# Second expert layer turned over (512 tokens move past w2 in split fp32r passes), scores spread by DMA, and batch 0's gate within attention step 15

## What is computed

```python
x = x + attention(ctx, layernorm(x))            # two batches of 512 tokens
x2 = layernorm(x)
probs = softmax(x2 @ Wg)                        # 8 experts
top_vals, top_idx = top_k(probs, 2)             # normalised to a sum of 1
scores = sum(onehot(top_idx) * top_vals)        # [tokens, 8], 6 of 8 are zero
h = relu(x2 @ W1[e] + b1[e])                    # per expert, 128 -> 256
y = h @ W2[e] + b2[e]                           # per expert, 256 -> 128
out = x + sum_e(y * scores[e])
```

## Time and profile before

| | |
|---|---|
| median of 3 runs | 345.25 us (345.12 to 345.28) |
| the profiled execution | 345.45 us, its span 343.7 us |
| busy: TensorE, VectorE, GpSimd, ScalarE | 98%, 79%, 74%, 56% of the span |
| granted TensorE clock | 1.00 of full |

### The profile page before, as it was taken

How to read it: one execution, slowest core, us unless ns; L and a number is a source line. 1 busy time by engine, 2 the same in 40 slices (tenths; PEclk the granted TensorE clock), 3 DMA queues, 4 the chain that set the end, 5 groups by cost and what they waited for, 6 DMA issues and landing times.

```text
span 343.7 us, 6136 instructions
## 1 busy us (share of the span) xinstructions
PE 336.9 (98%) x2355; PEld 231.9 (67%) x2355; DVE 270.7 (79%) x430; ACT 193.7 (56%) x257; POOL 254.1 (74%) x163
## 2 busy tenths in 40 slices
PE   7899999999999999999999999999999999999996
PEld 7576657584757566575847475665684478999896
DVE  5989757988999999999879897979728898267333
ACT  2564768484948566584849485665803544045341
POOL 4639999999999999999999899989883772110000
PEclk9999999999999999999999999999999999999999
DMA  4630000000010000000000000000000010000000
GB/s 126 212 97 0 2 0 4 0 17 0 2 31 17 15 2 0 3 1 2 0 17 2 1 0 17 0 2 0 2 3 0 1 32 0 2 0 2 31 3 31
DMA packets 6713, 5.81 MB, mean 17 GB/s; under 512 B 743, under 2 KB 5789, under 8 KB 6685
## 3 DMA queue, kind: packets, MB, share of 16 engines
q1 hardware_dynamic: 6389, 5.29, 5.0%
q10 hardware_dynamic: 296, 0.13, 0.1%
HBM read 4.89 MB, written 0.52 MB: 16 GB/s over the span
## 4 chain that ended last, share of the span: by engine, by line
PE 96%; ACT 2%; DVE 1%; issue 0%; POOL 0%; DVEq 0%; POOLq 0%
PE xo L415 25%; PE sc L395 21%; PE mx L617 8%; PE sc L401 6%; PE sc L321 6%; PE sc L322 5%; PE sc L323 5%; PE mx L352 3%; PE xo L352 3%; PE mx L504 2%; PE xo L504 2%; PE sc L436 2%; PE xo L424 2%; PE mx L321 1%; PE mx L322 1%; PE mx L323 1%
## 5 line engine op out<-in xcount | busy, mean ns | idle before, releaser
L1142 POOL TENSOR_TENSOR psum_acc<-psum_acc,probs 111x1024 f32<-111x1024 f32 x63 | 161.6, 2565 | 9.3 <-DVE psum_acc L864 1.9
L686 ACT ACTIVATE probs<-sc 111x1024 f32<-111x1024 f32 x96 | 98.2, 1027 | 19.0 <-PE sc L401 12.4
L415 PE MATMUL xo<-probs,v_sb 111*64 111x512 f32 x384 | 88.2, 596 | 0.0
L395 PE MATMUL sc<-q_pair,k_pair 64*111 64x512 f32 x576 | 86.0, 402 | 0.8 <-ACT v_sb L676 0.4
L395 PEld LDWEIGHTS sc<-q_pair,k_pair 64*111 64x111 f32 x576 | 44.7, 171 | 29.0 <-issue 12.2
L415 PEld LDWEIGHTS xo<-probs,v_sb 111*64 111x64 f32 x384 | 26.2, 137 | 42.3 <-issue 38.7
L875 DVE RECIPROCAL recips<-recips 128x128 f32<-128x128 f32 x64 | 54.0, 905 | 0.0
L841 DVE TENSOR_REDUCE part_max<-mx 128x2 f32<-128x888 f32 x32 | 34.7, 1083 | 18.3 <-PE mx L352 16.9
L1142 POOL TENSOR_TENSOR psum_acc<-probs 111x1024 f32<-111x1024 f32 x16 | 38.4, 2401 | 8.9 <-ACT probs L686 8.9
L702 ACT COPY recips<-xo 128x512 f32<-128x512 f32 x16 | 9.4, 587 | 56.7 <-PE xo L424 48.8
L401 PE MATMUL sc<-max_row,ones_r 64*111 64x512 f32 x192 | 38.2, 390 | 0.0
(11 more groups left out here) (179 smaller groups left out, 522.1 us busy)
## 6 DMA issues: line engine op xcount, KB each, us to landing
w_raw<-in_L_ffn_W SPq DMA_DIRECT2D x8, 128.0 KB, 2.3
x_tok<-in_x SPq DMA_DIRECT2D x2, 256.0 KB, 3.1
wv_raw<-in_L_xattn_Wkv SPq DMA_DIRECT2D x4, 128.0 KB, 2.8
wout_sb<-in_L_xattn_Wout SPq DMA_DIRECT2D x1, 512.0 KB
wqk_raw<-in_L_xattn_Wq SPq DMA_DIRECT2D x7, 64.0 KB, 1.9
wqk_raw<-in_L_xattn_Wkv SPq DMA_DIRECT2D x7, 64.0 KB, 2.4
out<-x_tok SPq DMA_DIRECT2D x1, 256.0 KB, 2.0
out<-x_tok SPq DMA_DIRECT2D x2, 128.0 KB, 1.7
```

The costliest lines, as they stand in the source:

```text
L395: pe.matmul(sc[0:KP, kt % 2, h, :], k_pair[r, s % QKB, k_part, at], q_pair[r, s % QKB, q_part, :], start=(k_part + q_part == 0), stop=False)
L415: mm = pe.matmul(o_ps[h * HD:(h + 1) * HD, :], v_sb[0:KP, s // 2 % 2, kt, at:at + HD], probs[0:KP, e % RING, h, :], start=(kt == 0), stop= ...
L686: act.activation(probs[0:KP, e % RING, :, :], sc[0:KP, kt % 2, :, :], ACT.Exp).then_inc(exp_done, 1)
L1142: pool.tensor_tensor(psum_acc[0:KP, s % 2, :, :], first, probs[0:KP, e % RING, :, :], ALU.add) \
```

## The change

The second expert layer is turned over. Before, the hidden tokens stood still and w2 moved; now parts of w2 stand still and 512 hidden tokens move, in fp32r. For that w2 is split into a high and a low part (ScalarE's `w2_high` in steps 11 to 14 into the buffers of the attention's weights, GpSimd's `w2_low`), and so is the hidden layer: for each expert ScalarE does `relu_first`, `high_first`, `relu_second`, `high_second`, GpSimd `low_first` and VectorE `low_second`. `layer_two(g)` is six passes of 512 columns, three for each half, and runs two experts behind `layer_one` (`LAG`).

The result now has features on partitions and tokens along the row, so the scores must be spread over all partitions: the turned scores go to DRAM (`score_rows`) and come back by eight DMAs, one per expert, each reading one row of 2 KB for 128 partitions (`spread`). `add_expert` is a multiplication (out of PSUM, into `scaled`) and an addition (both inputs in SBUF) of 128x512. At the end of a batch `turn_acc` transposes the sum back and `add_rows` adds it to x. The bias term is one matmul of 512 columns and enters with the first expert's addition.

Batch 0's gate moves into step 15: `turn_x2(0)` stands ahead of the dots of step 15 and `logits(0)` behind them, the transposes of the scores behind layer one of expert 0. VectorE leaves the reciprocals of steps 12 and 13 out of step 14, so that x1 comes first, and does them and those of 14 and 15 later; all five gathers of step 15 are GpSimd's. w1's high parts move from GpSimd to ScalarE, all of w1 is split by step 13. Of batch 1, `turn_scores(1)` stands at g = 10, `bias_term(1)` at 11, and `turn_acc` of batch 0 at 12. `out_project(1)` runs at g = 3 (seven pairs) and 4 (the last).

```diff
-W1_AT = {2: 0, 3: 1, 9: 2, 11: 3}
+W1_AT = {2: 0, 3: 1, 8: 2, 9: 3, 10: 4, 11: 5, 12: 6, 13: 7}
+W2_HI_AT = {11: (0,), 12: (1, 2), 13: (3, 4), 14: (5, 6, 7)}
 FR = 6
+LAG = 2
...
+        relu_ring = sb("relu_ring", [P, 2, N])
+        relu_lo = sb("relu_lo", [P, FR, N], F32R)
+        spread = sb("spread", [P, E, N])
+        relu_hi = sb("relu_hi", [P, FR, N], F32R)
...
+        score_rows = nc.dram_tensor("score_rows", (B, E, N), F32, kind="Internal").ap()
...
+            for b in range(B):
+                sp.wait_ge(score_copied, b + 1)
+                if b == 0:
+                    sp.wait_ge(added, (KT - 1) * STEPS)
+                sp.dma_start(score_rows[b], score_t[:, b, :]).then_inc(rows_out, 16)
+                sp.wait_ge(rows_out, 16 * (b + 1))
+                for e in range(E):
+                    if b:
+                        sp.wait_ge(y_scaled, e + 1)
+                    sp.dma_start(spread[:, e, :], score_rows[b, e].partition_broadcast(P)).then_inc(spread_in[e], 16)
+            sp.wait_ge(out_ready, 1)
...
+                pe.matmul(pj, b2_sb[:, :], score_t[:, b, :], start=True, stop=True).then_inc(bias_ready, 1)
...
+            def layer_two(g):
                 e = g % E
                 if g >= 2:
-                    pe.wait_ge(acc_v, QT * (g - 1))
+                    pe.wait_ge(y_scaled, g - 1)
+                elif g == 1:
+                    pe.wait_ge(score_copied, 1)
+                if g == B * E - 1:
+                    pe.wait_ge(r0_done, g)
+                pe.wait_ge(w2_split, min(g + 1, E))
+                for half, at in enumerate(halves if g == B * E - 1 else [slice(0, N)]):
+                    y = y_ps(g, half)[:, at]
+                    for c, hi_done, lo_done in ((0, hi0_done, lo0_done), (1, hi1_done, lo1_done)):
+                        n = (g * HC + c) % FR
+                        pe.wait_ge(hi_done, g + 1)
+                        pe.matmul(y, w2_hi(e)[:, c, :], relu_hi[:, n, at], start=(c == 0), stop=False)
+                        pe.matmul(y, w2_lo(e)[:, c, :], relu_hi[:, n, at], start=False, stop=False)
+                        pe.wait_ge(lo_done, g + 1)
+                        mm = pe.matmul(y, w2_hi(e)[:, c, :], relu_lo[:, n, at], start=False, stop=(c == HC - 1))
+                    mm.then_inc(y_ready, 1)
...
+            turn_x2(0)
             s = STEPS - 1
             for kt in range(KT):
                 dots(s, kt)
+            logits(0)
             pe.wait_ge(sum_copied, s - 1)
             total(s - 1)
-            for kt in range(3):
+            for kt in range(KT):
                 pv(s, kt)
-            turn_x2(0)
-            for kt in range(3, KT):
-                pv(s, kt)
-            logits(0)
             for g in range(B * E):
-                hidden(g)
+                layer_one(g)
+                if g == 0:
+                    turn_scores(0)
                 if g == 1:
+                    bias_term(0)
                     pe.wait_ge(o_copied, STEPS)
                     total(s, o_ps)
-                if g >= 1:
-                    expert_out(g - 1)
-                if g == 2:
+                if g == 10:
+                    turn_scores(1)
+                if g >= LAG:
+                    layer_two(g - LAG)
+                if g == 3:
                     pe.wait_ge(sum_copied, STEPS)
-                if g % E == 2:
-                    turn_scores(g // E)
-                if g % E == 3:
-                    bias_term(g // E)
+                    pe.wait_ge(o_norm, STEPS - 1)
+                    out_project(1, x1_ps[1], range(PAIRS - 1))
                 if g == 4:
-                    pe.wait_ge(score_copied, 1)
-                    out_project(1, x1_ps[1], range(PAIRS))
+                    pe.wait_ge(o_norm, STEPS)
+                    out_project(1, x1_ps[1], range(PAIRS - 1, PAIRS))
                 if g == 6:
                     turn_x2(1)
                 if g == 7:
                     logits(1)
-            expert_out(B * E - 1)
+                if g == 11:
+                    bias_term(1)
+                if g == 12:
+                    turn_acc(0, 0, range(QT))
+            for g in range(B * E - LAG, B * E):
+                layer_two(g)
+            for half in range(2):
+                turn_acc(1, half, range(2 * half, 2 * half + 2))
...
+            def relu_first(g):
+                if g >= 2:
+                    act.wait_ge(hi0_done, g - 1)
+                    act.wait_ge(lo0_done, g - 1)
+                relu(g, 0, relu_ring[:, g % 2, :], r0_done)
+
+            def high_first(g):
+                act.wait_ge(r0_done, g + 1)
+                if g >= 3:
+                    act.wait_ge(y_ready, g - 2)
+                act.copy(relu_hi[:, g * HC % FR, :], relu_ring[:, g % 2, :]).then_inc(hi0_done, 1)
+
+            def relu_second(g):
+                relu(g, 1, hid_ps[:, (g * HC + 1) % 4, :], r1_done)
+
+            def high_second(g):
+                act.wait_ge(r1_done, g + 1)
+                if g >= 3:
+                    act.wait_ge(y_ready, g - 2)
+                act.copy(relu_hi[:, (g * HC + 1) % FR, :], hid_ps[:, (g * HC + 1) % 4, :]).then_inc(hi1_done, 1)
...
-            copy_x2(0)
+                act.copy(score_t[:, b, :], score_ps[b][0:E, :]).then_inc(score_copied, 1)
+
+            gate_exp_of(0)
             copy_output(STEPS - 1)
-            gate_exp_of(0)
             act.wait_ge(added, (KT - 1) * (STEPS - 1) + 1)
             for g in range(B * E):
-                for c in range(HC):
-                    relu(g * HC + c)
+                relu_first(g)
+                high_first(g)
+                relu_second(g)
+                high_second(g)
+                if g in (0, 10):
+                    copy_scores(g // E)
                 if g == 1:
                     copy_sum(STEPS - 1, o_ps)
-                if g % E == 2:
-                    copy_scores(g // E)
                 if g == 6:
-                    copy_x2(1)
-                if g == 7:
+                    copy_x2()
+                if g == 8:
...
-                if s > HALVED:
-                    for c in range(RC):
-                        reciprocal(s - 1, c)
...
+            def low_second(g):
+                dve.wait_ge(hi1_done, g + 1)
+                if g >= 3:
+                    dve.wait_ge(y_ready, g - 2)
+                dve.tensor_tensor(relu_lo[:, (g * HC + 1) % FR, :], hid_ps[:, (g * HC + 1) % 4, :],
+                                  relu_hi[:, (g * HC + 1) % FR, :].bitcast(F32), ALU.subtract).then_inc(lo1_done, 1)
+
+            def add_expert(g, half=0, at=slice(0, N)):
                 b, e = g // E, g % E
-                dve.wait_ge(y_ready, g + 1)
-                if e >= 1:
-                    dve.wait_ge(acc_v, QT * g)
+                dve.wait_ge(y_ready, g + half + 1)
+                dve.wait_ge(spread_in[e], 16 * (b + 1))
+                if g == 0:
+                    dve.wait_ge(sum_ready, STEPS)
+                if g >= 2:
+                    dve.wait_ge(acc_v, g - 1)
+                dve.tensor_tensor(scaled[:, g % 2, at], y_ps(g, half)[:, at], spread[:, e, at], ALU.mult) \
+                   .then_inc(y_scaled, 1)
+                dve.wait_ge(y_scaled, g + half + 1)
+                if e == 0:
+                    dve.wait_ge(bias_ready, b + 1)
                 else:
-                    dve.wait_ge(score_ready, b + 1)
-                for t in range(QT):
-                    if g == B * E - 1 and t == 2:
-                        dve.wait_ge(y_ready, g + 2)
-                    dve.scalar_tensor_tensor(acc[:, b, t, :], y_ps(g, t)[:, t * P:(t + 1) * P],
-                                             score[:, b, t, e:e + 1], acc[:, b, t, :], ALU.mult, ALU.add) \
-                       .then_inc(acc_v, 1)
+                    dve.wait_ge(acc_v, g)
+                dve.tensor_tensor(acc_t(b)[:, at], scaled[:, g % 2, at], acc_t(b)[:, at] if e else pj,
+                                  ALU.add).then_inc(acc_v, 1)
...
             norm_x1(0)
-            gather(STEPS - 1, 3)
+            for c in range(RC):
+                reciprocal(STEPS - 4, c)
             split_x2(0)
             for c in range(RC):
-                reciprocal(STEPS - 2, c)
+                reciprocal(STEPS - 3, c)
             gate_start(0)
             gate_end(0)
+            dve.wait_ge(added, (KT - 1) * (STEPS - 1) + 1)
             for g in range(B * E):
-                add_expert(g)
+                low_second(g)
+                if g == 5:
+                    norm_x1(1)
                 if g < 2:
                     for c in range(2 * g, 2 * g + 2):
+                        reciprocal(STEPS - 2, c)
+                if g >= LAG:
+                    add_expert(g - LAG)
+                if g in (2, 3):
+                    for c in range(2 * g - 4, 2 * g - 2):
                         reciprocal(STEPS - 1, c)
-                if g % E == 3:
-                    add_bias(g // E)
-                if g == 3:
```

(42 more changed lines are left out.)

197 lines of the change are left out of this document (110 added, 87 removed).

## The result

The changed kernel takes **365.09 us** (median of 4 runs, 364.34 to 366.09) beside 345.26 for the kernel before in the same runs: ratio 1.0569, 95% interval 1.0548 to 1.059. Forecast were 358.4, from 348 to 363. The direction was right, the time lies 2 us above the range. The profiled execution took 365.76 us, its span is 364.0, 7.2 more than the 356.8 of the sum.

The account below looks back on a forecast made before the run. TensorE, busy 98% of the span, was taken as the bound. 340.3 us with nobody late plus waits of 7.2, 3.4, 1.8, 3.8 and 0.3 gave 356.8 of span; + 1.55 made 358.4 us, range 348 to 363.

Parts of the forecast that it names:

- the 356.8 of the sum: Whole kernel: span of 340.3 us with nobody late plus TensorE's forecast waits, 7.2 + 3.4 + 1.8 + 3.8 + 0.3.
- The mechanism that decides: Batch 0's gate in step 15: VectorE operations stand behind GpSimd's gathers, scores at 285.3, TensorE stands 7.2 us.
- no standing at the port: Rival, chance 0.15: short VectorE operations slip between GpSimd's, batch 0's gate ends at 276.6, time 348.2 us.
- Second layer and transposes: TensorE's experts: layer two 1.39 us for 1.78, 6.2 us off in all; turning batch 0's sum back costs 0.44.
- The bias term: On TensorE: one 512-wide matmul, two records of 0.215 us, replaces 1.08 us; 1.3 us off for both.
- The tail: After layer one of expert 15 (T): ScalarE, VectorE's last sums, transposes and store end at T + 10.7, 340.3 us.
- the span with nobody late: Whole kernel if no engine delays another: 340.3 us, which is 343.7 - 3.4.
- Batch 1's x1 and logits: TensorE waits 3.4 us before x2's transposes, norm tiles standing behind GpSimd low parts, and 1.8 us before the logits.
- Batch 1's scores: Before the scores' transposes TensorE stands 3.8 us; the gate takes 4.1 us and one standing, to 329.9.
- The spreads: Batch 1's scores through DRAM to all partitions take 5.2 to 6.6 us; TensorE waits 0.3 us (0 to 0.8).
- spreads are slow: Rival, chance 0.06: one-row reads for 128 partitions take twice the landing time, 3.1 us more in batch 1, about 361.5.
- a rival with 0.20: Chance 0.20: after TensorE's 7 us standing, pieces behind run at 1.2 GHz, up to 4.2 us more, 360.5 to 362.6.

Follow-up runs that it names:

- the last three kernels: Three edits plus both gates in PSUM, batch 1's cut in two, 346.39 us; then VectorE's last steps reordered, 345.57; then bias term and step 15's sum moved, 344.8.
- the tail turned round: Against the kernel with both gates in PSUM: at g = 14 and 15 VectorE multiplies the expert two back before the newest low part, adds behind; 345.57 us.
- the last version: Against the kernel with VectorE's last steps reordered: bias term and sum of step 15 moved behind the first second layer; 344.8 us, ratio 0.9982.
- the three-edit kernel: Changed kernel with batch 0's gate in PSUM, GpSimd held back from batch 1's norm tiles, x2's low part ahead of expert 6's; 352.46 us, ratio 1.0177.
- the first experiment: Changed kernel with 26 identity matmuls on TensorE ahead of the wait for batch 0's scores; 361.46 us, ratio 1.0464.

## Why the prediction was right in direction and short in size

*The mechanism that decides was right.* Forecast: VectorE's two-input SBUF operations in the gate stand until GpSimd's are over, gate some 13 us, TensorE 7.2 us idle. Measured: 12.4 and 6.50. The gate in PSUM takes 4.2 us in the same place, beside the same gathers. The Trainium skill ("SBUF — State Buffer", Who interferes with whom) tells of such a standing between these two engines; the trace agrees, with 12.4 us against 4.2. The rival *no standing at the port* (348.2) fell with it.

*Second layer and transposes* were right: 1.39 us an expert (351.07 to the start of the next piece at 352.46 by six records 0.23 apart), 0.44 for the transposes back.

*The bias term* was not. "Two records of 0.215" were to take 0.43 us in place of 1.08; the two records take 1.05 (342.48 to 343.53 above), so 0.03 is saved each time where 1.3 us were booked for the two. It is an fp32 matmul of 8 rows, and it was priced by the passes of layer one, which are fp32r; no run tells its type from its few rows.

*The tail* was T + 10.1 for T + 10.7 (353.9 to 364.0), 0.6 the other way. So the span with nobody late, forecast 340.3, is 341.0 in the kernel after and in the one with both gates in PSUM: right within 0.7, in part because two errors of opposite sign nearly cancel.

*Batch 1's x1 and logits*: 2.92 for 3.4 and 1.04 for 1.8; the tiles stood, 3.45 against 1.11.

*Batch 1's scores* were mis-sized: 5.25 for 3.8. The step gave the gate 4.1 us and one standing. In the trace it starts at 330.00, 0.5 before TensorE asks, and takes 5.67, because two of its operations stand beside expert low parts of GpSimd, 0.84 and 1.37:

```profile
330.43 0.84 DVE L1089 TENSOR_TENSOR g_prob<-g_exp,g_rec 128x32 f32<-128x32 f32 x1
...
332.50 1.37 DVE L1099 TENSOR_TENSOR g_eq<-g_eq,earlier 128x256 f32<-128x256 f32 x1
```

```profile
329.74 1.48 POOL L1265 TENSOR_TENSOR relu_lo<-relu_ring,relu_hi 128x512 fp32r<-128x512 f32 x1 [2.44 <-ACT relu_hi L871]
...
332.15 1.44 POOL L1265 TENSOR_TENSOR relu_lo<-relu_ring,relu_hi 128x512 fp32r<-128x512 f32 x1 [0.94 <-ACT relu_hi L871]
```

*The spreads* cost TensorE nothing in the changed kernel (forecast 0.3): the store of the scores is issued at 337.38, the first product starts at 342.07 and VectorE stands 3.88 us for it, but the low clock had made TensorE late too. With the clock up they cost 0.59 to 0.79 in the last three kernels. The rival *spreads are slow* had part of its premise right, 5.2 us from issue to landing for the 3.1 of the model, and no weight in the time.

*The step that failed* is the sum's: "340.3 + 7.2 + 3.4 + 1.8 + 3.8 + 0.3 = 356.8" holds no term for the clock. It stood beside as a rival with 0.20 and 2 to 4 us, on the ground that "nothing in rows speaks for it yet". The runs put in its place 5.25 us in batch 0 and 2.0 in batch 1, both removed where TensorE was kept busy. Two things were wrong in that rival besides its chance. It stopped at "layer one, bias, sum, layer one, 4.2 us" of work, where the low level lasted through 6.05 us of work by full clock (11.3 less 5.25), since bias term and sum did not bring it back. And it reckoned with one fall, although the sum had a second wait of 3.8 us. The Trainium skill ("TensorE: Matmul & The Clock Gate", Part 1: The HAM clock gate) was cited there; it sides with what the windows show, an array that stood being set back to the lower level and working there first. With 7.3 added, the sum gives 364.1 us of span beside 364.0. That it fits so well is luck in part: the waits were 0.8 shorter than forecast (15.71 for 16.2 + 0.3) and the tail 0.6, the bias terms 1.3 longer.

What the change is worth without its waits is 2.7 us of span (343.7 less 341.0), where 3.4 were forecast; the tail turned round takes 0.6 more. The kernel with both gates in PSUM gives all of it back to its waits of 2.75; the last version gets 0.6.

Open is why a wait of 2.9 us at x2 left the clock up in the kernel after and in the one with bias term and sum moved (both behind an earlier fall) and brought it down in three others, and whether the second group of runs at 347 is the fall behind the bias term that the trace of the three-edit kernel shows. No run of that group was profiled; that the group is gone when the two pieces are moved speaks for it, and so do its mean clocks (0.993 to 0.995 beside 0.996 to 1.0), while the 1.55 us that such a fall cost is less than the 2.5 by which the group is slower.

## What to carry to other kernels

A wait of several microseconds on TensorE is to be priced twice: the wait, and the work behind it at half clock until the granted clock is back, which light pieces put right behind the wait draw out (11.3 us against 4.6). A matmul is to be priced by a row of its own type and shape: two records of 512 columns took 0.46 us in layer one and 1.05 in the bias term. Short VectorE operations with both inputs in SBUF should not be set beside long GpSimd operations; with one input in PSUM they run undisturbed. A saving on the bounding engine reaches the end only if the engines that hand to it have the time to spare, so before taking 7 us from TensorE count how late each hand-over becomes, in a row, since a wait that is removed shows up again at the next one.

## What the hardware showed that was not expected

- The granted clock fell without any long wait: behind 0.60 us of waiting, the bias term of 8 rows and the sum of step 15 (1.12 and 1.08 us), to 0.50 from 283.2 to 286.9 in the three-edit kernel. In the kernel with batch 0's gate in PSUM alone the same pieces after the same wait kept 1.00.
- The same 2.9 us wait at x2 left the clock at 1.00 in the two kernels with a low stretch in batch 0 and was followed by 0.50 in the kernels that had no low stretch in batch 0.
- GpSimd's expert low part takes 1.25 to 1.31 us in most places and 1.43 to 1.51 beside VectorE's gate or adds, up to 1.77 in the last three kernels; an add of VectorE beside one took 1.81 for 0.69. The standing goes both ways.
- Executions of one kernel differ by 1.1 us before the attention starts: a group of six matmuls at 5.8 us took 0.94 us in the profile of the kernel after and 1.65 in that of the first experiment, with the granted clock recorded as 1.00 in both.
- A spread of one 2 KB row to 128 partitions (256 KB) lands 5.2 us after its issue as a median of the sixteen, issued eight in a row, with the DMA engines busy 0.99 of the time; one plain load of 256 KB takes 3.1.
